# Four graph layers on one core: 16 slots for gathered rows, 16 places for one-hots, and VectorE's tile work four steps later in its program

## The reference, cut to what matters

```python
h = relu(layernorm(x)); x = x + relu(segment_sum((h @ W0)[src] * edge_weight[:, None], dst))          # layer 0
h = relu(layernorm(x)); x = x + relu(segment_sum(norm[:, None] * (h @ W1.T + b1)[src], dst))           # layer 1
h = relu(layernorm(x)); x = x + (relu((h + segment_sum(h[src], dst)) @ G1 + g1) @ G2 + g2)             # layer 2
h = relu(layernorm(x)); x = x + concat_heads(segment_sum(alpha[:, None] * (h @ Ws + Wb)[src], dst))    # layer 3
```

## Time and profile before

| | us |
|---|---|
| median of 3 runs | 2626.45 (2623.59 to 2630.86) |
| span of the profiled execution, core 0 | 3086.3 |
| its time by the same measure as the median | not recorded; only its span is |
| PE busy | 2384.8 (77% of the span) |
| POOL busy | 1795.9 (58%) |
| DVE busy | 1593.7 (52%) |

### The profile page before, as it was taken

The page is one execution under the profiler, slowest core; times in us unless marked ns, Lnnn a source line. Parts: engine busy times, 40 slices in busy tenths (PEclk is TensorE's granted clock), DMA queues, the critical chain, the costliest instruction groups (busy, mean ns, idle before and its releaser), DMA issues.

```text
span 3086.3 us, 32808 instructions
## 1 busy us (share of the span) xinstructions
PE 2384.8 (77%) x8542; PEld 1265.4 (41%) x8542; DVE 1593.7 (52%) x3774; ACT 335.0 (11%) x523; POOL 1795.9 (58%) x1878
## 2 busy tenths in 40 slices
PE   7888889887678777785788888885068589988887
PEld 5534444343223222221354454453058445544444
DVE  7665555554234353332244444444059677766665
ACT  4200000000000000000000000001057310000000
POOL 0466666665466666665666666653710456666665
PEclk9898999998789888997899999997579789999999
DMA  6586666676567766666666666663134457776665
GB/s 157 174 243 180 174 180 177 187 241 177 154 192 212 203 201 205 196 193 181 184 200 198 204 200 199 204 181 80 10 101 153 136 157 211 208 222 192 194 190 171
DMA packets 212761, 557.12 MB, mean 181 GB/s; under 512 B 55433, under 2 KB 56834, under 8 KB 212601
## 3 DMA queue, kind: packets, MB, share of 16 engines
q0 software_dynamic: 144448, 462.60, 52.3%
q1 hardware_dynamic: 66970, 90.10, 9.7%
q10 hardware_dynamic: 1182, 2.33, 0.3%
HBM read 515.28 MB, written 39.59 MB: 180 GB/s over the span
## 4 chain that ended last, share of the span: by engine, by line
PE 51%; DVE 15%; another core or an unknown queue 13%; issue 12%; DMA 6%; POOL 2%; ACT 1%; SPq 0%; ACTq 0%; DVEq 0%; POOLq 0%
PE tiles L1456 28%; DMA ring<-table,src_t 5%; PE upper L1416 5%; PE last_bank L1597 2%; PE tiles L1453 2%; PE tiles L1452 2%; DVE sel L776 2%; PE upper L1458 2%; PE last_bank L1416 2%; PE upper L1687 1%; POOL ring L1758 1%; PE upper L1626 1%; PE upper L1405 1%; DVE stage L713 1%
## 5 line engine op out<-in xcount | busy, mean ns | idle before, releaser
L1758 POOL DMA_INDIRECT ring<-table,src_t x1320 | 1266.9, 960 | 717.8 <-issue 324.3
L1456 PE MATMUL tiles<-ring,sel 128*125 128x512 f32 x2590 | 1390.4, 652 | 264.2 <-issue 178.4
L1456 PEld LDWEIGHTS tiles<-ring,sel 128*125 128x125 f32 x2590 | 444.3, 198 | 754.6 <-issue 745.5
L1813 POOL DMA_INDIRECT ring<-table,src_t x415 | 399.0, 961 | 240.5 <-PE upper L1458 105.5
L483 DVE TENSOR_TENSOR sel<-iota_bank,dl_t 128x500 f32<-128x500 f32 (+1 forms) x330 | 221.5, 674 | 513.3 <-PE tiles L1456 226.6
L1218 DVE TENSOR_TENSOR ring<-ring,last_bank 128x512 f32<-128x512 f32 x388 | 260.5, 685 | 169.6 <-DMA ring<-table,src_t 140.6
L1458 PEld LDWEIGHTS upper<-big,sel 128*125 128x125 f32 x880 | 169.7, 193 | 222.5 <-issue 222.0
L1452 PE MATMUL tiles<-ring,sel 128*125 128x512 f16 x440 | 176.5, 401 | 61.8 <-issue 32.1
L1453 PE MATMUL tiles<-ring,sel 128*125 128x512 f16 x440 | 172.9, 393 | 10.6 <-issue 10.3
L1416 PE MATMUL upper<-wh,hTh 128*125 128x512 f32 x200 | 100.4, 502 | 73.1 <-DVE hTl L759 23.7
L1791 POOL DMA_INDIRECT big<-score_table,src_t x104 | 98.4, 946 | 81.5 <-DVE acc L988 50.1
(11 more groups left out here) (335 smaller groups left out, 2522.2 us busy)
## 6 DMA issues: line engine op xcount, KB each, us to landing
ring<-table,src_t POOLq DMA_INDIRECT x1735
table<-stage SPq DMA_DIRECT2D x50, 224.0 KB
table<-acc SPq DMA_DIRECT2D x50, 224.0 KB
acc<-dst_places SPq DMA_DIRECT2D x28, 256.0 KB
x<-dst_places SPq DMA_DIRECT2D x27, 256.0 KB
x<-in_x SPq DMA_DIRECT2D x25, 224.0 KB
kept_x<-x SPq DMA_DIRECT2D x25, 224.0 KB
x<-kept_x SPq DMA_DIRECT2D x25, 224.0 KB
```

The lines of the kernel that those rows point to most:

```text
L1456: last = P.matmul(to, sel[:, n % SELS, :], rows, start=False, stop=True, skip_group_check=True)
L1758: G.indirect_dma_start(out=(ring16 if layer == 2 else ring)[:, n % RING, :], out_offset=None, in_=table[layer][:, :], in_offset=bass.Indir ...
L1813: G.indirect_dma_start(out=rows_at(i), out_offset=None, in_=table[3][:, :], in_offset=bass.IndirectOffsetOnAxis(ap=src_t[:, i:i + 1], axis ...
```

## The change

`RING` is 16 instead of 11 and `SELS` 16 instead of 12. The memory for the five slots of 2 KB and the four places of 500 bytes in each partition comes from the descriptor area, which is 4 KB instead of 16. In layers 0 to 2 all the tile work on DVE is placed 4 steps later in DVE's loops. Three pieces that thereby fall behind the loop of layer 2 are called after it. PE's program is not changed, nor are `place_hots` (still at `DEG_STEPS[g]` + 4), the flags of layer 1, and the tile work of layer 3 (at E + 14).

```diff
-    RING = 11
-    SELS = 12
+    RING = 16
+    SELS = 16
...
-    Z_AT, Z_OUT = 59, 67
+    Z_AT, Z_OUT = 59, 71
...
-            for i in range(STEPS + 24):
+            for i in range(STEPS + 28):
...
-                k = ended.get(i - 12)
+                k = ended.get(i - 16)
...
-                k = ended.get(i - 18)
+                k = ended.get(i - 22)
...
-                k = ended.get(i - 22)
+                k = ended.get(i - 26)
...
-                k = ended.get(i - 14)
+                k = ended.get(i - 18)
...
-                for lag, work in ((14, split_sums), (24, first_bias), (30, second_bias), (35, first_relu), (45, new_rows),
-                                    (56, last_relu), (63, node_scores), (Z_OUT, rows_out)):
+                for lag, work in ((18, split_sums), (28, first_bias), (34, second_bias), (39, first_relu), (49, new_rows),
+                                    (60, last_relu), (67, node_scores), (Z_OUT, rows_out)):
...
+            rows_out(TILES - LATE - 1)
+            split_sums(TILES - 2)
+            first_relu(TILES - 3)
...
-    nc = bacc.Bacc("TRN2", target_bir_lowering=False, num_devices=1)
+    nc = bacc.Bacc("TRN2", target_bir_lowering=False, num_devices=1, dynamic_dma_scratch_size=4096)
```

## The result

The changed kernel takes 2668.8 us (median of 4, 2662.27 to 2676.83) beside 2628.05 for the kernel before: ratio 1.0159, 95% interval 1.0136 to 1.0183. It is 1.6% slower, some 41 us; I had forecast 2677.

A forecast was written before the change was run, and what follows sets the result against it. The prediction took PE and POOL to be near each other in layer 0, so added PE waits cost nearly in full. Its terms, 47.7 + 10.7 + 9 - 13 - 3, made +51 us, so 2677 us, range 2618 to 2712.

The forecast's parts named there:

- What bounds the kernel: Layer 0, timed runs: PE (527 us) and POOL near each other, so a wait added to PE costs nearly all of itself.
- The tile work, +47.7: Layer 0, tiles 2 to 16: DVE's later norm and split make PE wait about 2.8 to 3.3 us a tile, 47.7 us.
- tiles 0, 1 and 17, +10.7: Layer 0's other delayed tiles: DVE's later work makes PE wait +4.1, +2.1 and +4.5 us, together +10.7 us.
- The clock, +9: Layer 0's products: some run at the lower clock behind the new waits; +9 us, bounds 0 and 37.
- What the stretch gives back, -13: Layer 0: existing product waits and POOL being later cover part of PE's added waits; -13 us, bounds 0 and 23.
- Slots, -3: Start of layer 3: `RING` 16 lets five more gathers run ahead; -3 us, bounds -6.2 and 0.
- Layers 1 and 2, and the area: 0: `SELS` 16 with later tile work costs 0 there (layer 2 bounds -5 and +5); the smaller descriptor area costs 0.
- The signs in the profile: Layer 0: PE idle 40 to 60 us on DVE, tiles 2 to 17; POOL's gap 0.30 us; layer 3's seventeenth gather waits.
- A: Rival, chance 0.12: POOL sets layer 0's pace and covers the waits; 2626 ± 8 to 2650 us.
- C: Rival, chance 0.05: with the smaller descriptor area every gather pays, +0.1 us on 1735 gathers, 176 us; 2800 us.
- B: Rival, chance 0.15: deeper slots absorb POOL's pauses in all four layers, 70 us to be had; 2600 to 2620 us.
- D: Rival, chance 0.08: `place_hots` waits don't bind in layer 0, only layer 3's start gains; 2620 to 2632 us.

The follow-up runs named there:

- area_only: The kernel before with a descriptor area of 4 KB and nothing else; 2627.63 beside 2625.68 us, ratio 1.0007.
- hots_4_later: The changed kernel with `place_hots` 4 steps later too (`DEG_STEPS[g]` + 8); ratio to the kernel before 1.0033 on the slower chip, 0.9982 on a faster one.
- l0_shift_only_2: The kernel before with only layer 0's tile work on DVE 4 steps later, on a faster chip; 2679.02 beside 2625.56 us, ratio 1.0192.

## Why the prediction was right, point by point

- **What bounds the kernel.** Half wrong. I took the 460 us between profile and median to lie in the four layers and got 1.20 us a step, under POOL's 1.25. On the faster chips a gather still takes 1.25 us, layers 1 and 2 take 555 us at 1.26 a step, and layer 0 with all of before's waits 561. Of the 460 us some 144 lie outside the four layers: from the last step of layer 2 to the first of layer 3 it is 402.6 us in the profile before and 258.9 in `area_only`. The stretches of the earlier trace rows are also wider than the steps, which take 650, 626, 640 and 597 us there. So in layer 0 POOL is the later one in the kernel before, not PE. I also misread: that line names only the largest share. The full list of what ended POOL's waits in the first profile has PE in it, 208.5 us in 238 waits, 0.88 us each where 0.30 is the usual gap, so on the slower chip the slots did bind:

```profile
  issue: 324.3, 1015
  PE tiles L1456: 142.1, 171
  remote: 109.8, 64
  PE tiles L1453: 66.4, 67
```

- **The tile work, +47.7, and tiles 0, 1 and 17, +10.7.** The mechanism was right in its places; `hots_4_later` and `l0_shift_only_2` show it. The sum was 58.4 us, the added waits are 63.6: 53.6 in tiles 2 to 16, and 4.1, 2.1 and 3.8 in tiles 0, 1 and 17. A tile like tile 15 costs 2.44 + 1.47 = 3.9 us and not 3.3, mostly since I compared with a tile in which PE had lost 0.94 us already.
- **The clock, +9.** About right, though PE's busy time doesn't show it. Behind nine of the added waits, of 1.8 to 3.8 us, the granted clock went to the lower level: layer 0 has 34.9 us at that level in the changed kernel (52.8 in its second profile) and 12.5 in `area_only`. Behind others, as the 2.44 us of tile 15, it stayed at 1.00. Here are the transposes, three steps and a group of tile 15 and then of tile 16, the same work, PE alone (columns as the earlier trace rows):

```profile
544.23:549.35 5.12, 3.65 (x15) 1.00 0.76 215
568.80:573.92 5.12, 5.12 (x15) 0.67 0.72 202
```

  The second took 1.5 us more of PE's time, and saved the wait for the product that tile 15 has. Eight such stretches more than in `area_only`, less a shorter one at the start of the layer, make some 11 us, an estimate.
- **What the stretch gives back, -13.** This is the term that was mis-sized. Waits of 63.6 us and a clock of 11 would make 75 us; layer 0 grew by 41.4, so some 33 came back (an estimate, as the 11 is), above my bound of 23. Of these 20.6 us are idle time of PE's steps, mostly waits for gathers. The rest shows as busy time: PE was busy 1.6 us less in spite of the clock, and in the rows matmuls that don't wait overlap (a step's lasts 0.59 us and the next starts some 0.44 behind it), so that fewer waits between steps mean less busy time. The bound was too small because PE's own 527 us counted overlaps twice. By starts, a group costs 0.20 us and not 0.36, and the transposes 0.43 and not 0.59:

```profile
551.25 0.36 PE L1495 MATMUL upper<-big,stage 128*125 128x25 bf16 x4
551.45 1.96 PE L1456 MATMUL tiles<-ring,sel 128*125 128x512 f32 x4
...
555.74 0.59 PE L1405 MATMUL upper<-ident,stage 125*128 125x125 f32 x4
556.17 1.88 PE L1456 MATMUL tiles<-ring,sel 128*125 128x512 f32 x4
```

  So PE's own time was 505 us by the same sum, and POOL's 550 left 45 us to cover and not 23. The errors of the sum are +5 for the waits, +2 for the clock, -20 for this and +1 for the slots, together -12: 39 us for layers 0 and 3, where 51 were forecast; the medians differ by 41. That +7 and -20 partly cancel is luck.
- **Slots, -3.** In the changed kernel layer 3 gave 2 us; alone, 16 slots gave 9.5. The bound of 6.2 was too small by a little.
- **Layers 1 and 2, and the area: 0.** Right on the faster chips, to 1.5 us. On the slower one the later work and the 16 slots and places together cost 14 us, above the bound of 5 that I had set for layer 2.
- **The signs in the profile.** PE's idle time on DVE is 72.7 us, above the 40 to 60 that I had named. The rest is as said: no added wait from tile 18 on, POOL's gap 0.30 us, and in layer 3 the seventeenth gather into `ring` is the one that waits, 11.02 us.
- **Rivals.** A was right about the pace, but what it covers is less than half of the waits and the clock, and not most. C has nothing for it (0.1 us on 1735 gathers would have been 174 us, not 176). B's gain from depth is real but 10 us, not 70; against it I had the misread. The waits of `place_hots` did bind, against D: ahead of 90 of the 108 groups that wait DVE started within 0.1 us of the release.

## What to carry to other kernels

When work is moved later on one engine's program, look for what keeps that engine's lead over the other: here it was neither the slots nor the one-hots' places, both made deeper, but a small helper with two buffers at a fixed distance, and that distance has to move with the rest. Move all that is counted in the lead together, and check each wait that is left, with its release, against the step at which the consumer wants the result. Before sizing such a loss, find out which engine sets the pace without it, since the other engine's slack is subtracted once, and take that slack from starts and not from durations that overlap; and if the profile's span isn't the timed one, don't spread the difference evenly.

## What was unexpected of the hardware

The same kernel took 2626 us on two chips and 3087 on another, in each case within 0.7% over twenty runs and more. On the slower, a gather has its usual duration (949 ns against 946), and PE's busy time in layers 0 to 2 is 4 to 7% longer at the lower granted clock (0.892 against 0.961 for the whole). The larger part is that all engines stand idle more often. Many of these pauses end with a release for which the trace names no instruction ("remote"): POOL's gathers in layers 0 to 2 have 72 such waits, 102.5 us, on the slower chip and none on the faster ones. What makes them stand wasn't found, nor whether it is the chip or the occasion. A change that fits one kind needn't fit the other: 0.9982 and 1.0033 for the same kernel.

The clock is the other thing. Waits of 1.8 to 3.8 us at a tile's boundary, in a stretch that is busy otherwise, were followed by the lower level in nine cases of layer 0 and not in others of the same length (behind 2.44 us the granted clock was 0.71 in tile 13 and 1.00 in tile 15). PE's summed busy time hid the cost; it shows only when the same matmuls are compared.
